# The feature map of the chunk three ahead, moved to the front of VectorE's attention work

## The chip, the cores and the metric

One NeuronCore of one Trainium2 chip runs the whole kernel. The metric is the device time of one execution in microseconds. Its engines are TensorE (PE), VectorE (DVE), ScalarE (ACT), GpSimd (POOL) and SyncE (SP, which issues most DMAs). Each runs its own instruction stream in order, and they meet at semaphores only.

## The reference, cut to what matters

One layer over 2048 tokens of width 128: causal linear attention with 16 heads of 8, a layer norm, a mixture of 8 experts with two chosen for each token, and a layer norm.

```python
q = (x @ Wq.T).reshape(b, l, 16, 8)      # k and v alike
q = elu(q) + 1.0                         # the feature map; k too
k = elu(k) + 1.0
kv_cumsum = cumsum(einsum('blhd,blhe->blhde', k, v), axis=1)
k_cumsum = cumsum(k, axis=1)
out = einsum('blhd,blhde->blhe', q, kv_cumsum)
out = out / clip(einsum('blhd,blhd->blh', q, k_cumsum), 1e-6, None)[..., None]
x = layernorm(x + out.reshape(b, l, 128) @ Wo.T)
# router: rms norm, logits, softmax, top 2 of 8, weights renormalised and scaled
# experts: act = gelu(x @ gate0) * (x @ gate1); out = act @ linear_w, weighted and summed
x = layernorm(x + out)
```

## The kernel before

**Tiling.** The attention stage works on 16 chunks of 128 tokens, in groups of four. The group loop `groups` (L330) runs `step(g, m, route)` on every engine: m = -2 to 5 for group 0, then m = 2 to 5 for groups 1 to 3. In step m of group g, VectorE attends to chunk n = 4g + m - 1. From group 1 on, the four steps also carry `route` 0 to 3: pieces of the layer norm and the router of the group before. Groups 1 and 2 are one hardware loop.

**One chunk.** PE projects the chunk to q, k and v (`project`, L566, into PSUM). ScalarE's `inputs` (L778) makes exp(q,k) in `eqk`, relu(q,k) in `rqk`, and copies v to `v1` (act_in rises three times). VectorE's `features` (L983) waits for these three and writes `qk` = min(exp, 1) + relu, which is elu + 1 (L989, phi_done). GpSimd's `outer` (L475) waits for phi_done and writes the outer products `kv`, 1152 columns, into one of four buffers (L482, kv_done). PE's `prefix` (L573) transposes q and sums kv over the earlier tokens of the chunk by a triangular matmul in three parts (L583). VectorE's `attend` (L1002) multiplies these by q (`prod`, L1013, three operations, reading PSUM), sums over d (`num`, L1020), masks the state of the next chunk (L1000), adds the part that comes from earlier chunks (L1029, in PSUM), and computes den (L1034), its reciprocal rden (L1037) and o (L1041). PE turns o and multiplies by Wo (`turn_o`, `put_out`), and ScalarE copies y (`copy_y`).

**Who is ahead of whom.** Inside `attend` of chunk n, VectorE also does `features` of chunk n + 3; in the kernel before, behind the addition (L1029) and before `between(5)`. `between(i)` are nine places where pieces of the route are put: route 0 the mean negm (i = 1), the variance vare (4) and shift (8) of the group before, route 1 nothing, route 2 `choose` (zsqe at 1, then the logits, the two maxima and the indicators ind), route 3 `weigh_and_place` (esum at 0, prob and gw at 1, rank at 2, ..., combs at 6, slot at 8).

**What stands in which queue around it.** PE's step is: project chunk n + 3, prefix of chunk n, turn_o of n - 1, state of n, put_out of n - 1. In route 2 it is: prefix of n, project n + 3, `turn_z` (four transposes of zs, L615), state, logits, turn_o, put_out. At chunk 0 the projection of chunk 3 stands behind the prefix. A prefix part waits for the product of the same part of the chunk before (pre_used). ScalarE's step begins with inputs of chunk n + 3 and then copies qT and oT, except that in route 1 it is copy_qT, copy_oT, `normalise` (four activations to zs, L826; it waits for shift and rstd), `move_y`, inputs, and in route 2 copy_qT, `squares` (L839), copy_zT (L844), inputs. In route 3 the inputs stand behind exp_logits of route 2, which waits for VectorE's dlog. GpSimd's step is: in route 0 two scatters of the group before last, the power rstd (L487, waits for vare), then outer of chunk n + 3, and two more scatters; in route 2 the power rrms (L491, waits for zsqe), outer, four scatters; otherwise outer alone.

**Behind the attention stage** come the last scatters of rows to the experts' buffer in DRAM (L500, GpSimd, waiting for the slots of L1177), then 39 tiles of the experts, and the final layer norm.

Of the kernel before, what the change touches and what calls it, by code (L numbers as in the profile page):

```python
# [74 lines left out]
def build(nc, xT, x, wqkv, wo, rw, rscale, pes, gate_w, lin_w, consts, out):  # L75
# [4 lines left out]
    with ExitStack() as ctx:  # L80
# [245 lines left out]
        def exists(g, m):  # L326

            return not isinstance(g, int) or 0 <= GROUP * g + m < CHUNKS
# [20 lines left out]
        def after(eng, signal, count):  # L349

            if not (isinstance(count, int) and count <= 0):
                eng.wait_ge(signal, count)
# [615 lines left out]
        def _(ve):  # L968
# [11 lines left out]
            def heads(t, n=H):  # L980
                return t.rearrange("p (h e) -> p h e", e=HE)

            def features(g, m):  # L983

                n, s = GROUP * g + m, m % GROUP
                ve.wait_ge(act_in, 3 * (n + 1))
                after(ve, state_done, n - GROUP + 1)
                after(ve, kv_done, n - GROUP + 1)
                ve.scalar_tensor_tensor(out=qk[:, s, :], in0=eqk[:, m % 2, :], scalar=1.0, in1=rqk[:, m % 2, :],  # L989
                                        op0=ALU.min, op1=ALU.add).then_inc(phi_done, 1)  # L990

            def mask_state(g, m):

                n = GROUP * g + m
                if isinstance(g, int) and n < 1:
                    ve.wait_ge(state_zero, 1)
                else:
                    ve.wait_ge(state_done, n)
                after(ve, inter_done, n - 1)
                ve.tensor_tensor(state_m[:, m % 2, :], state_ps, const("block"), ALU.mult).then_inc(state_used, 1)  # L1000

            def attend(g, m, between):  # L1002


                n, s = GROUP * g + m, m % GROUP
                q = qk[:, s, 0:D].rearrange("p (h d) -> p h d", d=HD)
                for b, (h0, h1) in enumerate(HEADS):
                    ve.wait_ge(pre_done, 3 * n + b + 1)
                    if b == 0:
                        after(ve, summed, n)  # L1010
                    nh = h1 - h0
                    cols = nh * HE * HD
                    ve.tensor_tensor(  # L1013
                        prod[:, h0 * HE * HD:h1 * HE * HD].rearrange("p (h e d) -> p h e d", e=HE, d=HD),
                        pre_ps[b][:, 0:cols].rearrange("p (h e d) -> p h e d", e=HE, d=HD),
                        q[:, h0:h1, :].unsqueeze(2).to_broadcast([P, nh, HE, HD]), ALU.mult).then_inc(pre_used, 1)
                    between(b)
                ve.wait_ge(pre_used, 3 * (n + 1))
                after(ve, inter_used, n)
                ve.tensor_reduce(num[:, :], prod[:, :].rearrange("p (c d) -> p c d", d=HD), AX.X,  # L1020
                                 ALU.add).then_inc(summed, 1)
                between(3)
                if exists(g, m + 1):
                    mask_state(g, m + 1)
                between(4)
                ve.wait_ge(inter_done, n + 1)
                ve.wait_ge(summed, n + 1)
                after(ve, o_done, n)
                ve.tensor_tensor(inter_ps, inter_ps, num[:, :], ALU.add).then_inc(inter_used, 1)  # L1029
                if exists(g, m + 3):  # L1030
                    features(g, m + 3)
                between(5)
                ve.wait_ge(inter_used, n + 1)
                ve.tensor_scalar(den[:, :], heads(inter_ps)[:, :, HD], DEN_MIN, None, ALU.max).then_inc(den_done, 1)  # L1034
                between(6)
                ve.wait_ge(den_done, n + 1)
                ve.reciprocal(rden[:, :], den[:, :]).then_inc(rden_done, 1)  # L1037
                between(7)
                ve.wait_ge(rden_done, n + 1)
                after(ve, oTp_done, n - 1)  # L1040
                ve.tensor_tensor(o[:, m % 2, :].rearrange("p (h d) -> p h d", d=HD), heads(inter_ps)[:, :, 0:HD],  # L1041
                                 rden[:, :].unsqueeze(2).to_broadcast([P, H, HD]), ALU.mult).then_inc(o_done, 1)
                between(8)
# [157 lines left out]
            def step(g, m, route):  # L1201
                def between(i):
                    if route == 2 and i == 5 and is_last(g):
                        mean(g, 0, GROUP - 1)
                    if route is not None:
                        parts[route](g - 1, i)
                if route == 0 and (not isinstance(g, int) or g > 1):
                    ve.wait_ge(route_done, g - 1)
                if exists(g, m - 1):
                    attend(g, m - 1, between)  # L1210
                else:
                    if exists(g, m + 2):
                        features(g, m + 2)
                    if isinstance(g, int) and g == 0 and m == 0:
                        mask_state(0, 0)
                    for i in range(9):

                        if route == 3 and i == 2:
                            mean(g, GROUP - 1, GROUP)
                        if route == 3 and i == 5:  # L1220
                            mean_and_variance(g, 4)
                        if route == 3 and i == 8:
                            mean_and_variance(g, 8)
                            normalise_behind()
                        between(i)
# [179 lines left out]
```

## Time and profile before

| | |
|---|---|
| time, median of 3 runs | 228.59 us (228.45 to 231.94) |
| the profiled execution | 230.38 us, span 228.5 us |
| VectorE busy | 160.9 us, 70% of the span |
| PE busy | 158.9 us |
| GpSimd busy | 124.3 us |
| ScalarE busy | 101.1 us |
| feature map L989 | 16 times, median 0.416 us |
| kv L482 on GpSimd | 16 times, mean 2.17 us |

All times inside the trace are microseconds from the start of the span. A busy share is an average over stages, so what a change in the attention stage is worth is read from that stage's own timelines. A row of a timeline gives start, duration, engine, line, operation and tiles; in brackets stands the idle time of the engine before it and what ended it. An operation's duration includes the writing of its result, so the next one on VectorE can start before it has ended. A duration that is much longer than usual for its shape means that the operation was held after it had started.

### The profile page before, as it was taken

The page shows a single profiled execution, that of the slowest core. Times are in us where ns is not written, and L with a number is a line of the kernel's source. Part 1 is how long each engine was busy: PE and PEld are TensorE (multiplying, and loading weights), DVE is VectorE, ACT ScalarE, POOL GpSimd, SP SyncE. Part 2 cuts the span into 40 slices and gives each one's busy share as a digit, 9 for nine tenths or more (in the row PEclk, how much of TensorE's full clock was granted, in tenths as well). Part 3 has the DMA queues.
Part 4 walks back from the last instruction along what each step waited for, and adds up shares of the span by engine and source line. Part 5 has one row for each costly group of instructions (what it writes and reads, how often), then busy time and mean ns, then how long its engine had stood idle before and what let it go on. Part 6 is the DMA issues. An engine that isn't in the chain of part 4 may idle for free.

```text
span 228.5 us, 3949 instructions
## 1 busy us (share of the span) xinstructions
PE 158.9 (70%) x768; PEld 114.4 (50%) x769; DVE 160.9 (70%) x535; ACT 101.1 (44%) x359; POOL 124.3 (54%) x114
## 2 busy tenths in 40 slices
PE   2889989576785787675440006999999999971650
PEld 0446655353553545354330004878788888850430
DVE  0489999999989999999769911556655666621760
ACT  3315566472444723476540001556556666620270
POOL 5554643553348576447477750256566566661660
PEclk9999999999799977998555555899999999998575
DMA  5619600020000101010112533022323333215832
GB/s 158 211 27 313 269 17 0 0 80 11 1 23 12 58 12 35 26 71 25 67 51 73 149 94 93 14 79 81 80 82 97 83 82 92 71 46 134 269 96 65
DMA packets 19198, 18.54 MB, mean 81 GB/s; under 512 B 2944, under 2 KB 16256, under 8 KB 19056
## 3 DMA queue, kind: packets, MB, share of 16 engines
q1 hardware_dynamic: 16880, 13.69, 20.2%
q0 software_dynamic: 2304, 4.69, 6.2%
q8 instruction: 4, 0.07, 0.1%
q14 instruction: 10, 0.08, 0.1%
HBM read 10.60 MB, written 6.73 MB: 76 GB/s over the span
## 4 chain that ended last, share of the span: by engine, by line
PE 26%; issue 22%; DVE 18%; POOL 13%; DMA 8%; ACT 7%; DVEq 1%; SPq 1%; POOLq 1%; ACTq 0%
POOL zbuf L500 6%; POOL both L537 6%; DVE prod L1013 5%; PE bank L744 4%; PE bank L583 3%; DVE num L1020 3%; PE bank L570 3%; PE bank L733 3%; DMA both<-yout,zin 2%; PE bank L734 2%; PE bank L735 2%; DMA pl<-both 2%; DMA zin<-zbuf 2%; PE bank L773 2%; PE bank L752 2%
## 5 line engine op out<-in xcount | busy, mean ns | idle before, releaser
L537 POOL DMA_INDIRECT both<-yout,zin x39 | 37.3, 958 | 33.0 <-issue 16.6
L482 POOL TENSOR_TENSOR kv<-v,qk 128x1152 f32<-128x1152 f32 x16 | 34.8, 2174 | 30.6 <-DVE qk L989 30.6
L500 POOL DMA_INDIRECT zbuf<-rows,slot x32 | 32.6, 1018 | 13.7 <-issue 7.7
L583 PE MATMUL bank<-kv,C 128*128 128x432 f32 (+1 forms) x96 | 37.8, 533 | 2.5 <-DVE prod L1013 2.3
L583 PEld LDWEIGHTS bank<-kv,C 128*128 128x128 f32 x96 | 19.0, 212 | 18.8 <-issue 14.2
L1013 DVE TENSOR_TENSOR prod<-bank,qk 128x432 f32<-128x432 f32 (+1 forms) x48 | 24.8, 549 | 1.2 <-DVE slot L1177 0.5
L744 PE MATMUL bank<-w_l,actT 128*128 x156 | 24.7, 281 | 1.1 <-ACT actT L953 1.1
L724 PE MATMUL bank<-C,zin 128*128 128x128 f32 x39 | 11.4, 292 | 19.7 <-DMA zin<-zbuf 19.7
L744 PEld LDWEIGHTS bank<-w_l,actT 128*128 128x128 f32 x156 | 20.5, 190 | 8.9 <-issue 8.8
L1294 DVE COPY yout<-bank 128x128 f32<-128x128 f32 x39 | 11.4, 291 | 19.2 <-PE bank L744 19.2
L1020 DVE TENSOR_REDUCE num<-prod 128x144 f32<-128x1152 f32 x16 | 21.6, 1352 | 0.5
L948 ACT ACTIVATE gelu<-bank 128x256 f32<-128x256 f32 x39 | 14.9, 383 | 13.7 <-PE bank L735 13.7
L570 PE MATMUL bank<-w_qkv,xTs 128*128 128x384 f32 x32 | 17.1, 624 | 5.5 <-DMA xTs<-in_xT 3.5
L953 ACT COPY actT<-bank 128x256 f32<-128x256 f32 x39 | 14.5, 373 | 12.7 <-PE bank L752 12.7
L1279 DVE TENSOR_TENSOR zin_lo<-bank,zin_hi 128x128 fp32r<-128x128 f32 x39 | 11.4, 291 | 12.5 <-ACT zin_hi L943 8.6
L1287 DVE SCALAR_TENSOR_TENSOR act<-gelu,zin,bank 128x256 f32<-128x256 f32 x39 | 18.4, 472 | 2.3 <-ACT gelu L948 2.3
L733 PE MATMUL bank<-w_hi,zin_hi 128*128 x39 | 19.7, 505 | 0.0
L943 ACT CAST zin_hi<-bank 128x128 fp32r<-128x128 f32 x39 | 10.6, 271 | 20.0 <-PE bank L724 20.0
L724 PEld LDWEIGHTS bank<-C,zin 128*128 128x128 f32 x39 | 5.8, 148 | 20.5 <-DMA zin<-zbuf 20.4
L734 PE MATMUL bank<-w_lo,zin_hi 128*128 x39 | 16.0, 409 | 0.0
L735 PE MATMUL bank<-w_hi,zin_lo 128*128 x39 | 15.9, 408 | 0.0
L752 PE MATMUL bank<-C,act 128*128 128x128 f32 x78 | 15.1, 276 | 0.0
(152 smaller groups left out, 339.0 us busy)
## 6 DMA issues: line engine op xcount, KB each, us to landing
zin<-zbuf SPq DMA_DIRECT2D x39, 65.0 KB, 1.8
w_g<-in_gate_w SPq DMA_DIRECT2D x4, 512.0 KB, 5.9
pl<-both SPq DMA_DIRECT2D x8, 256.0 KB, 4.8
xTs<-in_xT SPq DMA_DIRECT2D x16, 64.0 KB, 2.2
w_l<-in_lin_w SPq DMA_DIRECT2D x1, 1024.0 KB, 9.1
zall<-zs SPq DMA_DIRECT2D x4, 256.0 KB, 2.4
out<-pl SPq DMA_DIRECT2D x8, 128.0 KB, 1.8
both<-yout,zin POOLq DMA_INDIRECT x39, 2.2
```

What stands on the lines that cost most here:

```text
L482: pool.tensor_tensor(kv[:, s, :].rearrange("p (h e d) -> p h e d", e=HE, d=HD), a, b, ALU.mult).then_inc(kv_done, 1)
L500: pool.indirect_dma_start(zbuf, bass.IndirectOffsetOnAxis(ap=slot_of(g)[:, c:c + 1].bitcast(U32), axis=0), rows_of(g)[:, j, r, :], None)\
L537: pool.indirect_dma_start(both, bass.IndirectOffsetOnAxis(ap=zin[:, b, D + 1:D + 2].bitcast(U32), axis=0), yout[:, b, :], None).then_inc(p ...
L570: pe.matmul(qkv_ps[:, 0:3 * D], xTs[:, m % GROUP, :], w_qkv[:, :], start=True, stop=True)\
L583: pe.matmul(pre_ps[b][:, 0:c1 - c0], const("tri"), kv[:, s, c0:c1], start=True, stop=True)\
L733: pe.matmul(g, zin_hi[:, b % 2, :], hi, start=True, stop=False)
L734: pe.matmul(g, zin_hi[:, b % 2, :], lo, start=False, stop=False)
L735: pe.matmul(g, zin_lo[:, b % 2, :], hi, start=False, stop=True).then_inc(gate_done, 1)
L744: mm = pe.matmul(yout_ps[b % 2][:, 0:D], actT[:, b % 2, h, :], w_l[:, bass.ds(e * (HB * D) + h * D, D)], start=(h == 0), stop=(h == HB - 1))
L752: mm = pe.transpose(actT_ps[b % 2][:, h * P:(h + 1) * P], act[:, b % 2, h * P:(h + 1) * P], const("ident"))
L1013: ve.tensor_tensor(prod[:, h0 * HE * HD:h1 * HE * HD].rearrange("p (h e d) -> p h e d", e=HE, d=HD), pre_ps[b][:, 0:cols].rearrange("p (h ...
L1020: ve.tensor_reduce(num[:, :], prod[:, :].rearrange("p (c d) -> p c d", d=HD), AX.X, ALU.add).then_inc(summed, 1)
```

## The change

The call of `features(g, m + 3)`, with its waits and its one instruction, moves from behind the addition of the numerator to the front of `attend`, before the wait for the first product. Nothing else is changed. Chunks 0 to 12 have such a call.

```diff
                 n, s = GROUP * g + m, m % GROUP
                 q = qk[:, s, 0:D].rearrange("p (h d) -> p h d", d=HD)
+                if exists(g, m + 3):
+                    features(g, m + 3)
                 for b, (h0, h1) in enumerate(HEADS):
                     ve.wait_ge(pre_done, 3 * n + b + 1)
                     if b == 0:
...
                 ve.wait_ge(summed, n + 1)
                 after(ve, o_done, n)
                 ve.tensor_tensor(inter_ps, inter_ps, num[:, :], ALU.add).then_inc(inter_used, 1)
-                if exists(g, m + 3):
-                    features(g, m + 3)
                 between(5)
                 ve.wait_ge(inter_used, n + 1)
```

## Rows read from the trace of the kernel before

**Rows 1.** The page: busy tenths of VectorE in 40 slices of the span
```profile
DVE  0489999999989999999769911556655666621760
```
**Rows 2.** Windows: us, busy (x) of PE, PEld, DVE, ACT, POOL; clock, DMA, GB/s
```profile
113.00:131.00 18.00, 3.60 (x16) 2.97 (x14) 14.58 (x70) 4.04 (x11) 14.12 (x14) 0.50 0.29 94
```
**Rows 3.** Source view of line 989: what ended VectorE's idle time before it
```profile
  ACT v L786: 2.0, 2
```
**Rows 4.** Timeline, chunk 2, a plain one: start, us, engine, line, operation
```profile
22.43 2.18 POOL L482 TENSOR_TENSOR kv<-v,qk 128x1152 f32<-128x1152 f32 x1 [2.51 <-DVE qk L989]
...
22.96 1.47 DVE L1013 TENSOR_TENSOR prod<-bank,qk 128x432 f32<-128x432 f32 x3
...
25.95 0.30 DVE L1029 TENSOR_TENSOR bank<-bank,num 128x144 f32<-128x144 f32 x1
26.17 0.41 DVE L989 SCALAR_TENSOR_TENSOR qk<-eqk,rqk 128x256 f32<-128x256 f32 x1
26.50 0.17 DVE L1034 TENSOR_SCALAR den<-bank 128x16 f32<-128x16 f32 x1
```
**Rows 5.** Timeline of VectorE, chunk 13, which has no features
```profile
96.56 0.32 DVE L1029 TENSOR_TENSOR bank<-bank,num 128x144 f32<-128x144 f32 x1
96.91 0.17 DVE L1034 TENSOR_SCALAR den<-bank 128x16 f32<-128x16 f32 x1
```
**Rows 6.** Timeline, chunks 0 and 1: ScalarE's last input of chunk 3, VectorE
```profile
15.97 0.28 ACT L786 ACTIVATE v<-bank 128x128 f32<-128x128 f32 x1
...
17.58 0.17 DVE L1034 TENSOR_SCALAR den<-bank 128x16 f32<-128x16 f32 x1
...
18.50 1.70 DVE L1013 TENSOR_TENSOR prod<-bank,qk 128x432 f32<-128x432 f32 x3
```
**Rows 7.** Timeline, from chunk 5's end (route 0) into chunk 6 (route 1)
```profile
41.39 2.08 DVE L1093 TENSOR_TENSOR shift<-negm,rstd 128x4 f32<-128x4 f32 x1
43.40 1.47 DVE L1013 TENSOR_TENSOR prod<-bank,qk 128x432 f32<-128x432 f32 x3
...
43.59 1.65 ACT L826 ACTIVATE zs<-y,shift,rstd 128x128 f32<-128x128 f32 x4 [1.43 <-DVE shift L1093]
...
46.08 0.28 ACT L786 ACTIVATE v<-bank 128x128 f32<-128x128 f32 x1
```
**Rows 8.** Timeline, PE, VectorE, ScalarE and GpSimd around chunk 7 (route 2)
```profile
44.05 2.20 PE L583 MATMUL bank<-kv,C 128*128 128x432 f32 x6 [1.15 <-DVE prod L1013]
46.42 0.91 PE L570 MATMUL bank<-w_qkv,xTs 128*128 128x384 f32 x2 [0.17 <-ACT v L786]
...
47.63 1.11 DVE L1013 TENSOR_TENSOR prod<-bank,qk 128x432 f32<-128x432 f32 x2
48.66 0.64 DVE L1104 TENSOR_SCALAR zsqe<-zsq 128x4 f32<-128x4 f32 x1
...
52.60 1.95 DVE L1053 TENSOR_TENSOR ind<-C,r_k 128x32 f32<-128x32 f32 x1
...
48.46 0.56 ACT L844 COPY zT<-bank 128x512 f32<-128x512 f32 x1
...
49.47 0.29 ACT L786 ACTIVATE v<-bank 128x128 f32<-128x128 f32 x1
...
49.38 1.01 POOL L491 TENSOR_TENSOR rrms<-zsqe,C 128x4 f32<-128x4 f32 x1
52.32 2.18 POOL L482 TENSOR_TENSOR kv<-v,qk 128x1152 f32<-128x1152 f32 x1 [1.93 <-DVE qk L989]
```
**Rows 9.** Timeline, chunk 8 (route 3) on VectorE, and a scatter of chunk 11's step
```profile
56.16 0.61 DVE L1013 TENSOR_TENSOR prod<-bank,qk 128x432 f32<-128x432 f32 x1
...
57.52 0.18 DVE L1053 TENSOR_TENSOR r_prob<-r_elog,r_einv 128x32 f32<-128x32 f32 x1
...
61.01 2.12 DVE L1053 TENSOR_TENSOR r_combs<-r_comb,pes_b 128x32 f32<-128x32 f32 x1
...
87.06 0.96 POOL L500 DMA_INDIRECT zbuf<-rows,slot  x1 [0.31 <-issue]
```

## The prediction

> **What bounds the kernel now.** I read the page's 40 slices first [rows 1]: VectorE is at eight or nine tenths or more from the third slice to the nineteenth, about 11 to 108 us (a slice is 5.7 us), and at nine in all but two of them. That is the attention stage, and its speed there is VectorE's. The table of windows comes next [rows 2]: in the 18 us behind it GpSimd is busy for 14.12 us with scatters that wait for the last slot numbers. They come from VectorE, so a delay of the attention stage goes through to the end one for one; I found nothing behind it that absorbs it. Then the view of line 989, the feature map [rows 3]: VectorE waits for ScalarE before it only 2.0 us in two places, both in the start-up. In its old place the feature map is never late. The timelines of the four engines, read side by side for one step of each kind, give all the rest.
>
> I number the chunks 0 to 15. VectorE attends to chunk n and computes the features of chunk n+3 in the same piece of work. A step of the group loop carries a route number 0 to 3 from g = 1 on: chunks 5 and 9 are route 0, 6 and 10 route 1, 7 and 11 route 2, 8 and 12 route 3. Chunks 0 to 4 have none. Chunks 13 to 15 issue no features.
>
> **What the change does.** 13 feature maps (chunks 0 to 12) move ahead of the three products, the sum, the mask and the addition. The count of instructions stays, and no DMA is moved. Two things move with each: the wait for ScalarE's three input operations of chunk n+3 (all VectorE work of the chunk is queued behind it), and the release of GpSimd's kv product, 2.2 us.
>
> **1. The cover behind the addition goes.** In a plain chunk the addition starts at 25.95, the features at 26.17, den at 26.50: 0.55 us from addition to den [rows 4]. In the chunks without features it is 0.35 (96.56 to 96.91) [rows 5], since den waits for the addition's result. So taking the features out saves 0.21, and putting them at the front costs 0.33 (26.17 to 26.50). Net +0.12 us for each of the chunks 2, 3, 4. In routes 2 and 3 other small operations stand between, so the full 0.33 comes back there and the move costs nothing.
>
> **2. Chunk 0.** ScalarE ends the inputs of chunk 3 at 15.97 + 0.28 = 16.25; PE projects chunk 3 only behind chunk 0's prefix matmuls. The products of chunk 0 would start at 16.28 + 0.33 = 16.61. In a plain chunk den comes 3.54 us behind the first product (22.96 to 26.50) [rows 4], 3.33 without the features between: 19.94, against 17.58 now [rows 6]: +2.36. Chunk 1's products waited for PE some 0.2 us before them and 0.2 inside (1.70 long at 18.50, against 1.47 at 22.96) [rows 4, 6]; PE isn't later in the new order, so that wait goes and pays for chunk 1's features at the front, and with the 0.21 saved behind its addition +2.03 is left. With 0.36 for chunks 2 to 4: +2.39. In those chunks the inputs end a little under 1 us before the new place, by an estimate that shifts ScalarE's and PE's timelines along with chunk 0's delay.
>
> **3. Route 0 (chunks 5, 9).** GpSimd stands at rstd before kv, so kv doesn't move ahead: VectorE's shift, normally 0.16 us, is again held until kv ends (2.08 us, 41.39 to 43.47) [rows 7]. Its end hangs on the variance behind negm and ScalarE's squares, so what is saved behind the addition doesn't count. At chunk 5 negm is no longer held by an earlier kv and gives 0.28 of the 0.33 back: +0.05. At chunk 9 it wasn't held: +0.33.
>
> **4. Route 1 (chunks 6, 10): the main term.** ScalarE's inputs of chunk n+3 stand behind the normalisation of the group, and that waits for the very shift that ends the VectorE piece before. Shift ends at 43.47, the four zs start at 43.59, v ends at 46.08 + 0.28 = 46.36 [rows 7]. The old order had the products running from 43.40; the new one starts the features at 46.39 and the products at 46.72. That is 3.32, less 0.21 from point 1: +3.1 each, 6.2 for both.
>
> **5. Route 2 (chunks 7, 11).** PE's prefix for chunk 7 waits for the first product of chunk 6, so it moves from 44.05 to about 47.35. PE then does the matmuls (1.95 to 2.2 us), the projection (0.75, from 46.42 to 47.17) and the four transposes of zs (0.6), to about 50.7 to 50.9, and only then can ScalarE copy zT and do the inputs behind it. From the copy's start to the end of v is 49.47 + 0.29 - 48.46 = 1.30 [rows 8]. So the features can start at 52.0 to 52.3; VectorE would be there at 50.75 (the old front at 47.63 and 3.1). A stall of 1.4 and 0.33 for the features: +1.73. Against that, inside the piece: zsqe (0.64) is not held by kv, -0.48; the features are gone from the middle, -0.33. GpSimd has rrms before kv: kv now starts right behind rrms, 2.3 us after the first product, not behind the features. It then meets r_logit in place of ind and holds it 1.6 where ind was held 1.8 (1.95 long) [rows 8], -0.15. Net +0.8 each, 1.6 for both.
>
> **6. Route 3 (chunks 8, 12).** The old kv held r_combs 2.12 us instead of 0.17: 1.95 lost. The new kv runs from about 0.5 to 2.7 us after the features' start. The products read PSUM and are not held (three took 1.47 with a kv beside them [rows 4]); r_prob, 1.36 behind the first product (56.16 to 57.52) [rows 9], so 1.69 behind the features, is held about 1.0. Chunk 8: -0.95. At chunk 12 four scatters, 0.96 and 0.31 each [rows 9], stand before kv in GpSimd's queue. Counted from chunk 11's first product, kv starts at 2.3 (rrms done) + 2.2 (its own kv) + 5.0 = 9.5. VectorE's r_gw starts at 8.53 (47.63 to 56.16) - 0.96 + 0.33 + 1.36 + 0.22 = 9.48. If it gets past, only 0.3 is lost at r_reng: -1.65. If it is held, 2.1 is lost: +0.15. I take the first and keep the second for the range.
>
> **Sum.** 2.03 + 0.36 + 0.05 + 3.1 + 0.8 - 0.95 + 0.33 + 3.1 + 0.8 - 1.65 = 8.0 us. The profiled execution took 230.38 (span 228.5), 1.8 above the median of 228.59. On its own time the sum gives 238.4, on the median **236.6 us**, 3.5% slower.
>
> **A rule weighed against the rows.** ind's 1.95 us ended with a kv (to 54.55; kv ran 52.32 to 54.50) [rows 8], whereas the products, with an operand in PSUM, took 1.47 beside the kv of 22.43 to 24.61 [rows 4]. The Trainium skill, "SBUF — State Buffer", section "Who interferes with whom", says that an operation of VectorE with two inputs in SBUF needs the interface that it shares with GpSimd, and is blocked for the whole of a GpSimd instruction that reads SBUF. The trace agrees. By this rule alone the change looks good: kv is put under the PSUM products, where it disturbs nobody. The first rival follows this thought.
>
> **Rivals.** (a) Not slower: the inputs are ready at the new place wherever they are asked for, and only the collisions change. For it: VectorE never waits at line 989 past the start-up [rows 3]. Against: ScalarE's queue, where v ends at 46.36 and the place is now 43.40 [rows 7]. It decides where v ends before the front of the chunk; each us by which it is late costs one. Price: the sum without the stalls of routes 1 (2 x 3.0) and 2 (2 x 1.4), 8.0 - 8.8 = -0.8; without chunk 0's too, -2.8: 225.8 to 227.8 us. (b) Only the first stall of each group: ScalarE catches up while VectorE waits, and route 2's inputs are ready. For it: v ended at 49.76, well ahead of its use behind the addition [rows 8]. Against: the transposes of zs on PE, behind prefix matmuls that wait for the products. Price 8.0 - 2.8 = 5.2: 233.8 us. (c) More than the sum: r_gw of chunk 12 is held (+1.8), and the inputs of chunk 12, only some 0.2 us ahead of the front of chunk 9 by my sum, are late, or PE's prefix runs slower after its longer waits: the windows show a granted clock of 0.50, its level of 1.2 GHz, where PE is busy for a fifth of the time [rows 2], and each longer wait of VectorE is one of PE's too. Up to +3.4: 240 us. (d) Nothing: the collisions pay for the stalls. All holds by kv together, about 12 us, would have to go, but shift's two (3.8) and route 2's (3.2) stay, as rstd and rrms stand before kv in GpSimd's queue. Price near 229 us.
>
> **How the numbers follow.** Forecast with (b) and (c) as its edges: 0.87, of which (b) 0.08 and (c) 0.14; (a) 0.06; (d) 0.05; anything else 0.02. The likeliest is the sum, 236.6. The range is 233.8 (b) to 240.0 (c), which leaves out (a), (d) and what lies past (c). A measurement of this kernel tells about 2% (4.6 us) from no change: slower by more than that 0.87, within it 0.10, faster by more 0.03.
>
> **What would show it.** In the profile after, line 989 waits for ScalarE's v: about 3 us at chunks 6 and 10, about 1.4 at 7 and 11, a few us at chunk 0 (point 2, 4, 5); nothing at 1 to 5. Shift is still about 2.1 long (3). zsqe is short, r_logit or its neighbour is long instead of ind (5). r_combs is short and r_prob about 1.2 (6). Features to products is 0.33 and addition to den 0.35 in plain chunks (1). The scatters' tail starts about 8 us later and is as long as before. I would be wrong if ScalarE's inputs of routes 1 and 2 ended before the front, or if the wait at line 989 was less than 1 us in all past chunk 0.

## The result, and the profile after

| | before | after |
|---|---|---|
| median of the runs shown | 228.84 us | 245.33 us |
| all runs | 228.45 to 231.94 | 243.77 to 246.62 |
| the profiled execution, its span | 230.38, 228.5 | 245.75, 243.9 |

The ratio is 1.072, 95% interval 1.065 to 1.079: 16.5 us slower. The sign was forecast, the size was not: 236.6 us, at most 240.0.

The page of the changed kernel, VectorE's busy tenths and PE's granted clock in 40 slices (before the change VectorE stood at nine almost throughout, [rows 1]):

```profile
DVE  0449998465988549998986894155666666640571
...
PEclk9999999759959869759965555579999999999586
```

VectorE now has holes, at slices 8 to 10 and 14 to 15, and PE's clock falls in or just behind them. The source view of line 989 gives the holes a name (idle time of VectorE before the line, us, times):

```profile
  ACT v L786: 20.6, 8
```

It was 2.0 in two places [rows 3]. The timeline of VectorE shows six of the eight (the other two are in the start-up, as before). Columns as in the rows of before:

```profile
16.29 0.42 DVE L989 SCALAR_TENSOR_TENSOR qk<-eqk,rqk 128x256 f32<-128x256 f32 x1 [3.38 <-ACT v L786]
...
43.61 2.13 DVE L1093 TENSOR_TENSOR shift<-negm,rstd 128x4 f32<-128x4 f32 x1
48.66 0.43 DVE L989 SCALAR_TENSOR_TENSOR qk<-eqk,rqk 128x256 f32<-128x256 f32 x1 [2.92 <-ACT v L786]
...
57.35 0.42 DVE L989 SCALAR_TENSOR_TENSOR qk<-eqk,rqk 128x256 f32<-128x256 f32 x1 [4.22 <-ACT v L786]
...
60.55 1.63 DVE L1053 TENSOR_TENSOR r_logit<-lgs,rrms 128x32 f32<-128x32 f32 x1
...
67.04 0.82 DVE L1053 TENSOR_TENSOR r_prob<-r_elog,r_einv 128x32 f32<-128x32 f32 x1
...
73.44 0.43 DVE L989 SCALAR_TENSOR_TENSOR qk<-eqk,rqk 128x256 f32<-128x256 f32 x1 [1.02 <-ACT v L786]
...
83.73 0.43 DVE L989 SCALAR_TENSOR_TENSOR qk<-eqk,rqk 128x256 f32<-128x256 f32 x1 [2.92 <-ACT v L786]
...
91.96 0.43 DVE L989 SCALAR_TENSOR_TENSOR qk<-eqk,rqk 128x256 f32<-128x256 f32 x1 [3.76 <-ACT v L786]
...
101.48 2.58 DVE L1053 TENSOR_TENSOR r_prob<-r_elog,r_einv 128x32 f32<-128x32 f32 x1
```

Chunk 0 (3.38), chunk 6 (2.92), chunk 7 (4.22), chunk 9 (1.02), chunk 10 (2.92), chunk 11 (3.76). Those of chunks 0, 6 and 10 are as large as I had them. Those of 7 and 11 were to be 1.4. (L1015 and L1031 of the changed kernel are L1013 and L1029 of the one before.)

PE around chunk 7 (in [rows 8] the same prefix took 2.20 us; behind the projection's start the transposes came after 0.75 us, here after 1.28; they took 0.6):

```profile
49.66 4.21 PE L583 MATMUL bank<-kv,C 128*128 128x432 f32 x6 [4.69 <-DVE prod L1015]
53.66 1.49 PE L570 MATMUL bank<-w_qkv,xTs 128*128 128x384 f32 x2
54.94 1.02 PE L615 MATMUL bank<-C,zs 128*128 128x128 f32 x4
```

And windows of it (us, busy (x) of PE, PEld, DVE, ACT and POOL, granted clock, DMA share, GB/s):

```profile
36.00:44.70 8.70, 6.96 (x34) 4.37 (x32) 7.85 (x19) 4.43 (x19) 2.63 (x3) 1.00 0.00 0
44.70:49.60 4.90, 0.27 (x3) 0.03 (x1) 1.98 (x4) 3.55 (x14) 1.45 (x2) 0.59 0.14 54
49.60:53.70 4.10, 4.04 (x7) 2.23 (x8) 3.39 (x9) 1.04 (x6) 1.74 (x1) 0.50 0.11 32
```

PE is at 2.4 GHz until it waits for VectorE's product. In the wait the clock falls, and the whole prefix runs at 0.50, which is 1.2 GHz. It takes twice its time.

Where the time came, by the start of each chunk's first product (us; the forecast is worked out from the prediction's own terms):

| chunk | before | after | later by | of it new in this step | forecast of the step |
|---|---|---|---|---|---|
| 2 | 22.96 | 25.38 | 2.42 | 2.42 | 2.36 |
| 6 | 43.40 | 49.00 | 5.60 | 3.18 | 3.40 |
| 7 | 47.63 | 57.69 | 10.06 | 4.46 | 1.5 |
| 8 | 56.16 | 65.69 | 9.53 | -0.53 | -0.6 |
| 9 | 65.02 | 73.78 | 8.76 | -0.77 | -0.95 |
| 10 | 71.91 | 84.08 | 12.17 | 3.41 | 3.3 |
| 11 | 76.14 | 92.31 | 16.17 | 4.00 | 1.5 |
| 12 | 84.69 | 100.13 | 15.44 | -0.73 | -0.6 |
| 13 | 93.09 | 108.86 | 15.77 | 0.33 | -2.0 |

The row of chunk 13 holds chunk 12's own piece. Three steps carry the error: chunk 7 (2.9), chunk 11 (2.5) and chunk 12's own piece (2.3).

Behind this table 1.06 us more are lost inside chunk 13's piece: chunk 14's first product starts at 97.86 before and at 114.69 after, 16.83 later. VectorE waits there for PE, whose prefix for chunk 13 took 3.73 us, at a granted clock of 0.50 between 104.90 and 110.30:

```profile
110.25 0.61 DVE L1015 TENSOR_TENSOR prod<-bank,qk 128x432 f32<-128x432 f32 x1 [0.78 <-PE bank L583]
```

The last slot numbers are 16.83 later too (121.93 and 138.76), so up to them the delay went through one for one, as forecast. The last scatter starts at 134.60 before and at 150.35 after, only 15.75 later, because two scatters of the trace before took 1.50 us in place of 0.96:

```profile
129.73 1.50 POOL L500 DMA_INDIRECT zbuf<-rows,slot  x1 [0.31 <-issue]
```

Such long scatters come in some traces (none in the changed kernel's, up to two in others, whatever the version). That this gave the 1.06 us back is luck of the two executions.

### The profile page after: what moved, and what is told of

It reads as the page before. It is cut to its first block, busy times and chain, and to the rows that moved or that the text cites. A ratio compares the mean times of both kernels' runs of the same rounds, so it can differ in the third digit from the quotient of the medians.

```text
span 243.9 us, 3951 instructions
## 1 busy us (share of the span) xinstructions
PE 162.5 (67%) x768; PEld 117.0 (48%) x769; DVE 159.3 (65%) x535; ACT 101.2 (41%) x359; POOL 123.2 (51%) x114
## 4 chain that ended last, share of the span: by engine, by line
PE 28%; DVE 19%; issue 18%; POOL 14%; DMA 8%; ACT 8%; SPq 1%; DVEq 1%; POOLq 1%; ACTq 0%
PE bank L583 6%; POOL zbuf L500 6%; POOL both L537 6%; DVE prod L1015 4%; PE bank L744 4%; PE bank L570 3%; DVE num L1022 3%; PE bank L733 2%; DMA both<-yout,zin 2%; DMA pl<-both 2%; PE bank L735 2%; PE bank L734 2%; ACT zs L826 2%; DVE shift L1093 2%; DMA zin<-zbuf 2%
## 5 line engine op out<-in xcount | busy, mean ns | idle before, releaser
L583 PE MATMUL bank<-kv,C 128*128 128x432 f32 (+1 forms) x96 | 41.7, 580 | 9.4 <-DVE prod L1015 9.4
L500 POOL DMA_INDIRECT zbuf<-rows,slot x32 | 31.5, 984 | 20.0 <-ACT rows L864 10.4
L583 PEld LDWEIGHTS bank<-kv,C 128*128 128x128 f32 x96 | 20.5, 229 | 26.9 <-issue 14.8
L1015 DVE TENSOR_TENSOR prod<-bank,qk 128x432 f32<-128x432 f32 (+1 forms) x48 | 24.6, 550 | 1.1 <-PE bank L583 1.0
L989 DVE SCALAR_TENSOR_TENSOR qk<-eqk,rqk 128x256 f32<-128x256 f32 x16 | 8.6, 540 | 20.8 <-ACT v L786 20.6
L570 PE MATMUL bank<-w_qkv,xTs 128*128 128x384 f32 x32 | 17.6, 640 | 5.1 <-DMA xTs<-in_xT 3.5
```

What stands on the lines that cost most here:

```text
L500: pool.indirect_dma_start(zbuf, bass.IndirectOffsetOnAxis(ap=slot_of(g)[:, c:c + 1].bitcast(U32), axis=0), rows_of(g)[:, j, r, :], None)\
L570: pe.matmul(qkv_ps[:, 0:3 * D], xTs[:, m % GROUP, :], w_qkv[:, :], start=True, stop=True)\
L583: pe.matmul(pre_ps[b][:, 0:c1 - c0], const("tri"), kv[:, s, c0:c1], start=True, stop=True)\
L1015: ve.tensor_tensor(prod[:, h0 * HE * HD:h1 * HE * HD].rearrange("p (h e d) -> p h e d", e=HE, d=HD), pre_ps[b][:, 0:cols].rearrange("p (h ...
```

## The experiments

Two theories at the start. A: the excess is PE's clock, which falls in the wait that route 1 makes, so that route 2's inputs come late a second time. B: the chain prefix, projection, transposes, zT copy, inputs is as long as it is by its order, and the clock is beside the point.

**Filler on PE in route 2.** PE is kept busy in its wait; nothing else of the changed kernel is touched, save that the addition of the chunk before waits for the last filler, since both use that PSUM bank.

```diff
+                if route == 2:
+                    keep_busy(6, 18).then_inc(filled, 1)     # 18 x identity @ identity into B[6][:, 384:512]
                 for b, (h0, h1) in enumerate(HEADS):
...
+                if route == 1:
+                    ve.wait_ge(filled, g)
                 ve.tensor_tensor(inter_ps, inter_ps, num[:, :], ALU.add).then_inc(inter_used, 1)
```

> The changed kernel, with 18 matmuls of no use (identity times identity, into a free part of a PSUM bank, about 4 us) put where PE stands idle for 4.7 us before the prefix of chunks 7 and 11; the addition of the chunk before waits for the last of them, long after it is done. Theory A (PE's clock): the excess over my sum is that PE, idle for 4.7 us, comes back at its lower clock, so that prefix, projection and the transposes of zs take twice as long. Then the prefix of chunk 7 takes 2.1 to 2.2 us and not 4.21, the wait of VectorE for the inputs of chunks 10 and 14 falls from 4.2 and 3.8 to about 1.5, and the kernel takes about 240 us (245.3 - 2 x 2.6). Theory B (the order on PE alone, not its clock: prefix, projection and transposes are as long as their dependencies make them): the filler changes nothing, 245 us, or makes it slower by what it overhangs.

Measured: 244.61 us, ratio to before 1.068 (1.062 to 1.073). The time is B's, the trace is A's. The prefix of chunk 7 took 2.20 us, the waits of chunks 7 and 11 fell to 1.20 each, and chunk 12's first product started 5.6 us earlier against that of chunk 2 than in the changed kernel. But in the last group, where no features wait, the filler itself was in the way: chunk 14's addition waited 2.33 us for the last of it, and its piece took 6.48 us instead of 4.05. So the filler was left out there:

```diff
-                if route == 2:
+                if route == 2 and not is_last(g):
...
-                if route == 1:
+                if route == 1 and not is_last(g):
```

> The changed kernel with the 18 filler matmuls only in front of the prefixes of chunks 7 and 11, no longer of chunk 15, where VectorE doesn't wait for inputs and the filler itself made PE late (the piece of chunk 14 took 6.5 us instead of 4.05). Theory A (the clock of PE after its long wait makes the excess in route 2): the wait at the features of chunks 7 and 11 is 1.2 again, and the 3 us lost in the last group come back: 239 to 240 us. Theory B (the filler of e1 gained nothing in sum): 243 to 245 us.

Measured: 239.20 us, ratio 1.043 (1.039 to 1.047), where the changed kernel has 1.072. About 6 us of the 16 go away by work of no use on PE. In the traces, 3.0 and 2.6 us of this are in the steps from chunk 6 to 7 and from chunk 10 to 11. The profiled execution also had a start-up 1.3 us shorter, which isn't the filler's doing (chunk 2 at 24.05 in place of 25.38, with the same code up to there), and lost 0.6 us at chunk 9 in a new wait for PE. Timelines of PE and VectorE, and the window of the filled wait:

```profile
43.47 4.18 PE L576 MATMUL bank<-C 128*128 128x128 f32 x36
48.33 2.20 PE L592 MATMUL bank<-kv,C 128*128 128x432 f32 x6 [0.68 <-DVE prod L1024]
50.37 0.81 PE L571 MATMUL bank<-w_qkv,xTs 128*128 128x384 f32 x2
51.01 0.60 PE L624 MATMUL bank<-C,zs 128*128 128x128 f32 x4
```
```profile
53.00 0.42 DVE L998 SCALAR_TENSOR_TENSOR qk<-eqk,rqk 128x256 f32<-128x256 f32 x1 [1.20 <-ACT v L795]
```
```profile
43.30:48.30 5.00, 4.35 (x39) 4.16 (x38) 2.08 (x4) 3.58 (x14) 1.55 (x2) 1.00 0.14 52
```

The product it waits for comes just as late; only the clock differs. From chunk 6 to chunk 7 the piece is now 5.67 us, 1.44 longer than before, and my forecast was 1.5. Theory A holds for route 2, and the rest of point 5 with it.

**Filler in route 3 too.** PE has two more waits there (3.4 and 2.9 us). In the first run the filler behind the ranks was written with start=True into the bank in which the running state adds up; this changes the state, so that run computes another attention and is read for its timeline alone. In the second it is added with start=False and leaves the state alone.

```diff
+                    if route == 3 and b == 2:
+                        keep_busy(4, 14)                 # in prefix, before the third part
...
                     ranks(g - 1)
+                    pe.wait_ge(state_used, GROUP * g + m)
+                    keep_busy(5, 12)                     # second run: start=False
                     pe.wait_ge(rank_used, g)
```

> As the one before, and filler in PE's two idle stretches of route 3 as well: 14 matmuls inside the prefix of chunks 8 and 12, 12 behind the ranks. Theory A: the state, the output and the next projection after them run at the higher clock, ScalarE's y and the inputs of chunk 12 come earlier by about 1 us, and the 1.02 us that VectorE waits before chunk 9's features go too: about 239 us. Theory B: 245 us, and the 1.0 us stays, being the held r_prob or the order of ScalarE's queue.

> The one before, with filler in route 3 too (14 matmuls inside the prefix of chunks 8 and 12, 12 behind the ranks, the latter added to an unused part of the state's bank). Theory A: the wait of 1.02 us before the features of chunk 9 is gone as in the first such run (0.55 was left, of another kind), and the sum of what is left is near my predicted one: 238 to 239 us. Theory B: no difference to the kernel without filler in route 3.

Measured: 241.37 us, ratio 1.056 (1.048 to 1.063), against 1.068 of its sister without filler in route 3; then 1.032 (1.025 to 1.039) against 1.043. The second ratio rests on two of the run's four executions. In both traces the wait of 1.02 us for chunk 12's inputs is gone. In its place stands a wait behind the slots, 0.55 us, which the kernel before had as well (0.48). It stands where the hardware loop turns from group 1 to group 2 and is missing at chunk 13; what it is was not looked into. The row is the first run's:

```profile
68.90 0.42 DVE L1002 SCALAR_TENSOR_TENSOR qk<-eqk,rqk 128x256 f32<-128x256 f32 x1 [0.55 <-DVE slot L1192]
```

So that wait was PE's clock too, 0.5 us of it. The intervals of each pair meet at their ends; the traces carry this reading more than the times do. The loss inside chunk 13's piece is gone as well: PE's clock is 1.00 from 98.30 to 103.00 in the second run, the prefix takes 2.10 us, and chunk 14 starts 4.76 us behind chunk 13, where it was 4.77 before and 5.83 in the changed kernel.

With both fillers the kernel is 3.2% slower than before, and my 8.0 us were 3.5%. That the two are so near is luck in part: in the trace chunk 13 starts 9.02 us later than before (102.11), since r_prob is still held for 2.58 us at chunk 12. But step by step the second run bears the sum out: 1.99, 3.19, 1.43, -0.54, -1.23, 3.33, 1.44 and -0.72 us for the first eight rows of the table, none off by more than 0.4, and 0.13 for the last, where -2.0 was forecast. With PE kept at 2.4 GHz, that one step is all that is wrong.

**One part of the move at a time.** `attend` is told its route, and the call stands in front only where the condition holds, else in its old place:

```diff
+                front = route == 1
+                if front and exists(g, m + 3):
+                    features(g, m + 3)
                 for b, (h0, h1) in enumerate(HEADS):
...
                 ve.tensor_tensor(inter_ps, inter_ps, num[:, :], ALU.add).then_inc(inter_used, 1)
+                if not front and exists(g, m + 3):
+                    features(g, m + 3)
```

> The feature map stands at the front in route 1 only (chunks 6 and 10), everywhere else in its old place. Theory A: +3.1 us each for the wait, and PE's prefix of chunk 7, released late, runs at the lower clock, so the logits of the group come late and VectorE waits about 2 us for them in route 2 although its features are back behind the addition: +4.5 to 5 each, 238 us. Theory B: route 2 absorbs the delay of PE at the full clock, +2.6 each, 234 us.

Measured: 238.84 us, 1.038 (1.031 to 1.045), 8.8 us. Of this 2 x 3.1 are the waits at line 989. The rest is the echo in route 2, at another place, since the features don't stand in front there:

```profile
54.27 0.19 DVE L1056 TENSOR_TENSOR r_logit<-lgs,rrms 128x32 f32<-128x32 f32 x1 [1.15 <-ACT lgs L856]
```

and 2.00 us at chunk 11. PE's prefix took 4.21 again, behind a wait of 4.50 (46.81). Whoever looked at line 989 alone would miss it.

> The feature map stands at the front in route 2 only (chunks 7 and 11). PE's prefix isn't delayed here, so both theories have its clock high. By the trace of before, v of chunk 10 ends at 49.76 and the front is at 47.63: a wait of 2.15, 0.33 for the features, less 0.48 (zsqe no longer held), 0.33 and 0.15: +1.5 each, 231.8 us. If a wait of 2 us costs much more than this even without the late prefix, theory A is not what makes route 2 long.

Measured: 232.23 us, 1.011 (1.005 to 1.016), 2.4 us; 2.08 us of wait at each of the two places where 2.15 was worked out.

The same with `front = route in (1, 2)`:

> The feature map at the front in routes 1 and 2 (chunks 6, 7, 10, 11), elsewhere in its old place. If the excess over my sum is PE's low clock behind the wait of route 1, as theory A says, it is all here: +3.1 and +4.5 at chunks 6 and 7, +3.1 and +4.1 at 10 and 11 as in the changed kernel, less what route 3 gives: 13 to 15 us slower than before, 242 to 244 us, of the 16 in all. Rival (it comes about only together with the moves of chunk 0 or routes 0 and 3): the waits are 2.9 and 1.4 and the kernel takes 237 us.

Measured: 240.56 us, 1.053 (1.043 to 1.062), 12.0 us. Waits of 2.92 and 3.51 at chunks 6 and 7, 2.93 and 3.34 at 10 and 11. The two routes by themselves give 8.8 + 2.4 = 11.2, so they very nearly add up, and three quarters of the 16.4 are here. I had expected 13 to 15; the clock rose earlier here (the projection behind the slow prefix took 1.15 and 0.99 us, in the changed kernel 1.49 and 1.40, and the transposes of zs 0.60 both times), so the second waits were 0.4 to 0.7 shorter. The excess in route 2 doesn't need the moves elsewhere.

The same with the front at chunk 0 alone:

> The feature map at the front at chunk 0 only. Theory A (my point 2): the wait for v of chunk 3 (to 16.25) costs 2.4 us at chunk 0, and chunk 1's wait for PE, some 0.4 us, is gone, with no features at its front to eat that up: +2.0 us, 231.2 against 229.2 before. Rival: the start-up has slack that gives it back in chunks 1 to 4: within 0.5 us of before.

Measured: 230.86 us, 1.015 (1.004 to 1.026), 3.4 us; by the interval alone it could be 1.0 or 5.9. The trace says more. The wait was 3.37 and den came at 19.73, close to the 19.97 of the changed kernel. But 1.43 us more were lost at chunk 7, at r_logit, for lgs. PE:

```profile
45.76 4.21 PE L583 MATMUL bank<-kv,C 128*128 128x432 f32 x6 [1.15 <-DVE prod L1016]
```

The wait before this prefix was 1.15 us, no longer than in the kernel before [rows 8], and yet it ran at the low clock. Against the kernel before, chunk 2's first product is 1.71 us later (24.67) and chunk 8's 3.25 (59.41), and nothing is given back: the rival falls. So 2.0 were about right for the wait of chunk 0, and what came on top was the clock again, in a place where nothing had changed but the moment at which it comes.

**Route 3, which should gain.** The front at chunks 8 and 12 alone:

> The feature map at the front in route 3 only (chunks 8 and 12), elsewhere in its old place. The inputs are ready 0.5 us before the front. Theory A (my point 6): kv now runs under the products and the sum; r_combs is no longer held (1.95 less), r_prob is held 0.8 to 1.0: -1.0 at chunk 8 and -0.3 at chunk 12: 1.3 us faster than before, about 0.6%. Rival: what is taken from r_combs is given back in full at r_prob or r_reng, no difference; or r_prob is held for 2.4 us at chunk 12 as in the changed kernel, 1 us slower.

Measured: 229.14 us, 1.000 (0.996 to 1.005): no difference. Here VectorE is 1.15 us earlier at the slots of chunk 8, as forecast, but the next products then wait for PE:

```profile
64.86 0.61 DVE L1016 TENSOR_TENSOR prod<-bank,qk 128x432 f32<-128x432 f32 x1 [1.46 <-PE bank L583]
66.19 0.61 DVE L1016 TENSOR_TENSOR prod<-bank,qk 128x432 f32<-128x432 f32 x1 [0.72 <-PE bank L583]
```
```profile
63.18 3.46 PE L583 MATMUL bank<-kv,C 128*128 128x432 f32 x6
```

PE is released by the copy of the rank. The hold of r_combs fell behind that copy, the hold of r_prob (1.03 long) stands ahead of it and moves it from 58.31 to 59.44. So kv's 2 us were taken off a stretch in which PE was at work, and PE, for the most part at the low clock once more (3.46 for the prefix), had become the bound.

**A version built from this.** What pays is to take kv off shift in route 0. The features stand in front in routes 0 and 3; in route 0 negm is computed ahead of them, and GpSimd does kv before rstd.

```diff
-                front = ...
+                front = route in (0, 3)
+                if route == 0:
+                    mean(g - 1, 0, GROUP)                # no longer at between(1)
...
-                if route == 0:
-                    if g >= 2:
-                        scatter(g - 2, (0,))
-                    norm_pow(g - 1)
...
                 if exists(g, m + 2):
                     outer(g, m + 2)
+                if route == 0:
+                    norm_pow(g - 1)
                 if route == 0 and g >= 2:
+                    scatter(g - 2, (0,))
                     scatter(g - 2, (1,))
```

> A candidate for a better version. Features at the front in routes 0 and 3, old place elsewhere. In route 0 the mean negm goes ahead of the features, GpSimd does kv before rstd, and its scatters behind both. Theory A: kv of chunks 8 and 12 runs under the products of chunks 5 and 9, where nothing is held, so shift is 0.16 and not 2.1 us long (-1.9 each), the variance's chain starts 1.3 us earlier: with route 3's -1.3 about 5 us faster than before, 223 to 225 us, 2%. Rival: rstd stands behind kv and comes so late that shift waits for it instead, or the scatters moved behind it delay kv of route 1: no more than 1.3 us faster.

Measured: 226.30 us, ratio to before 0.986 (0.981 to 0.990), 3.3 us faster than before (1.4%; the interval lies wholly below 1) and 8% faster than the changed kernel. Shift is 0.16 us long:

```profile
40.51 1.03 POOL L487 TENSOR_TENSOR rstd<-vare,C 128x4 f32<-128x4 f32 x1 [0.90 <-DVE vare L1090]
```
```profile
41.58 0.16 DVE L1095 TENSOR_TENSOR shift<-negm,rstd 128x4 f32<-128x4 f32 x1
```

Of the expected 5 us, 1.4 went at chunk 5, where the kv before now holds negm (1.58 us), and 1.1 at chunk 11, where kv stands behind four scatters and holds zsqe (1.76). Two tries to keep more, the first with route 3's features back in their old place, the second with one pair of scatters in route 2 and r_prob one place later:

> The part of the candidate (e8_r0_r3_kv_first) that stands in route 0, with route 3's features in their old place. Theory A: the candidate's gain of 3.3 us is shift, no longer held by kv: 2 to 3 us faster than before, 226.5 to 227.5. Rival: route 3's front is needed for it: no faster than before.

> The candidate, with two small moves. The scatters of one row block go from route 0 to route 2 on GpSimd, so that kv of route 1 doesn't stand behind four scatters and zsqe of chunk 11 isn't held for 1.76 us; and r_prob and r_gw go one place back, behind the third product, where kv has almost ended. Expected: 1.1 us from the first and 0.6 at chunk 8 from the second, 224.5 to 225 us. Rival: six scatters in a row make kv of chunk 15 late and hold as much in route 3: 226.3 as the candidate.

Measured: 226.83 us, 0.993 (0.989 to 0.998), and 226.86 us, 0.995 (0.991 to 0.999). Both are faster than before. Neither shows a gain over the candidate, and whether the three differ can't be told, since they weren't all timed on one occasion and the kernel before moved by 1.6 us between the two (229.41 and 227.79). In the second, kv of chunk 15 stood behind six scatters, and comb took 2.80 us, to kv's end, the rival's case.

## Why the prediction was wrong

Point 1 (cover behind the addition) was right: features to products 0.34 (16.29 to 16.63), addition to den 0.34. Point 2: the wait came as worked out; den at 19.97 against 19.94. So close a fit is luck of two executions with the same start-up: with the front at chunk 0, chunk 2's first product starts between 24.05 and 25.38 in the six traces, with the old order between 21.59 and 22.96 in the eight. But the means, 24.70 and 22.35, are 2.35 apart, and 2.36 was forecast. Point 3: shift 2.13 long, vare's chain as long as before. Point 4, the main term: features at 48.66, 2.92 behind the end of shift, and 3.2 us for the step where 3.4 were forecast.

**Point 5 failed**, and it is one term of it. "PE then does the matmuls (1.95 to 2.2 us), the projection (0.75) and the four transposes (0.6)": the work and its order were right, the durations were read from a PE at 2.4 GHz. I had just let PE wait for some 4.5 us in my own sum (1.15 and 3.3) and didn't ask what clock it would come back with. They took 4.0, 1.28 and 1.02 at chunk 7 and 4.0, 1.24 and 0.60 at chunk 11, 2.8 and 2.3 us more than the longest that I had; the steps missed by 2.9 and 2.5. I had named the cause in case (c), but within 3.4 us for everything in it, of which 1.8 were r_gw's, and gave (c) 0.14. The 1.6 left were a guess that no row stood behind; by the run with filler the clock cost 5.6 at these two places. The rest of point 5 held: zsqe 0.16 long, r_logit held for 1.63 in place of ind, and with PE kept busy a wait of 1.20.

The Trainium skill, "TensorE: Matmul & The Clock Gate", section "Why this matters for your kernels", warns that idle stretches of PE between bursts of matmuls bring the half rate back. The windows above agree (clock 1.00, then 0.59 in the wait, then 0.50). The prediction left this rule out of its sum. PE isn't the bound of this kernel, yet it stands in the chain that feeds ScalarE and through it VectorE.

**Point 6** was right for chunk 8: r_combs 0.18, r_prob held for 0.6 where I had 1.0. It failed for chunk 12, where r_gw was to get past kv by 0.02 us. r_prob itself was held, 2.58 us, to the end of kv:

```profile
100.83 0.96 POOL L500 DMA_INDIRECT zbuf<-rows,slot  x1 [0.30 <-issue]
101.81 2.19 POOL L482 TENSOR_TENSOR kv<-v,qk 128x1152 f32<-128x1152 f32 x1
```

By the sum's own times r_prob would start 0.24 us ahead of kv, and it did start 0.33 ahead (101.48, 101.81); I took what starts first to get past. The term that failed is this order: r_prob was 2.4 us longer than its usual 0.18, where I had 0.3 at r_reng, so 2.1 us, the second part of the miss (the rest of that step's 2.3 is a wait for PE, 0.24). With only 0.02 us between r_gw and kv it should have counted half to each side in any case. The long hold also kept PE waiting 4.16 us for the ranks, from which it came back at the low clock: that is the 0.24 and the 1.06 inside chunk 13's piece, and with filler in that wait both are gone. Chunk 9's inputs, "only some 0.2 us ahead", were late by 1.02, in good part by PE's clock, as the filler in route 3 shows; against the wait for the slots that stood there before, and with a shorter hold of r_prob, this step missed by 0.2.

By the table: 8.0 + 2.9 + 2.5 + 2.3 + 0.2 = 15.9, with 15.77 measured at chunk 13. The 1.06 us behind it are a further miss, which the scatters' 1.08 happened to cover.

Rival (a) fell with the first wait, (b) with the second. The rule of the Trainium skill that the prediction weighs ("SBUF — State Buffer", section "Who interferes with whom") was right as a rule: kv under the products held nobody there (three took 1.48 at 49.00, with a kv from 49.16 to 51.33). But it priced the side effect of the move and not its main effect.

## What to carry to other kernels

Moving a wait to the front of an engine's piece of work costs the lateness of its producer as the queues stand at that very point: read the producer's queue there, step kind by step kind, not the average wait of the line in its old place. When a sum makes another engine wait longer, go on and ask what that engine's next durations will be; for PE take them at the low clock as one bound, at each place where it waits and not only at the first. A gain is worth something only if the engine next in line isn't already at its limit, as route 3 showed.

## What the runs showed of the hardware

PE's clock fell not only behind waits of 4.5 to 4.7 us. At chunk 7 it was high behind a wait of 1.15 us in the kernel before and low behind a wait of the same 1.15 us in the run with chunk 0 alone (prefix 2.20 and 4.21 us). The 4.9 us of work ahead of the two waits were alike as well (PE busy for 3.53 and 3.54 us, clock 1.00). What decides between the two is open; no run here was made to find out.

An operation of VectorE with both inputs in SBUF was held although its row starts before that of GpSimd's kv: r_prob at 101.48, kv at 101.81, r_prob's end at 104.06, kv's at 104.00. With its usual 0.18 us r_prob would have been done before kv's row starts. The same showed in the four runs with filler (in one, 95.28 for 2.57 us, kv at 95.60) and at comb in the last run (86.31 for 2.80 us, kv at 86.82). Each time the operation started during the scatter just ahead of that kv. A scatter alone didn't hold such an operation: r_eq at 97.17 took 0.19 us beside the scatter of 96.95 to 98.01. Whether kv's hold begins earlier than its row, or it needs a scatter just before, is open.
